# A rebuilt opening: layer 0's wider weights in two transfers, the first half rounded between the two Gelus

## The reference, cut to what matters

```python
x = x + ffn0(conv(x, cond_128, ...))       # x: (128, 32, 512); conv: 9 taps, 4 groups, plus a bias from cond_128
x = x + ffn1(mix(x, cond_128, ...))        # mix: a 32x32 matrix for each sample
# mix: h = gelu(c @ W0 + b0); h = gelu(h @ W1 + b1); att = softmax(h @ W2 + b2)   (8 kernels)
#      agg_w = att * weight (a matrix for each sample);  out = agg_w @ x + att @ bias_k
# ffn: logits = y @ W_router.T; the two best of 8 experts, softmax of the two as weights w
#      h = y @ A.T (8 experts x rank 16);  out = y @ W_base.T + b_base + SCALING * (h * w) @ B
...
```

## Time and profile before

| | |
|---|---|
| median of 3 runs | 398.42 us (396.69 to 398.55) |
| the profiled execution | 398.19 us, span 396.4 us |
| PE busy | 386.1 us (97%), 2789 matmuls |
| DVE, ACT, POOL busy | 280.5 (71%), 207.4 (52%), 226.6 us (57%) |
| share of TensorE on the chain that ended last | 90% |

### The profile page before, as it was taken

The page is one execution under the profiler, slowest core; times in us unless marked ns, Lnnn a source line. Parts: engine busy times, 40 slices in busy tenths (PEclk is TensorE's granted clock), DMA queues, the critical chain, the costliest instruction groups (busy, mean ns, idle before and its releaser), DMA issues.

```text
span 396.4 us, 9115 instructions
## 1 busy us (share of the span) xinstructions
PE 386.1 (97%) x2789; PEld 376.2 (95%) x2789; DVE 280.5 (71%) x983; ACT 207.4 (52%) x529; POOL 226.6 (57%) x199
## 2 busy tenths in 40 slices
PE   7989999999999999999999999999999999999996
PEld 6668999999999999999999999999999999999995
DVE  2787776767667776766777676677767667776764
ACT  3847455555445555544555554455555445555541
POOL 3387765555566565556656555665655566565560
PEclk9999999999999999999999999999999999999999
DMA  7871212222221122222111222212212221121101
GB/s 248 294 157 55 79 49 62 63 73 80 80 80 51 56 66 67 80 80 80 53 54 57 75 80 80 80 53 53 65 67 80 80 80 55 51 70 63 56 27 55
DMA packets 19821, 31.04 MB, mean 78 GB/s; under 512 B 5920, under 2 KB 6208, under 8 KB 19808
## 3 DMA queue, kind: packets, MB, share of 16 engines
q1 hardware_dynamic: 19808, 30.89, 25.2%
HBM read 21.97 MB, written 8.91 MB: 78 GB/s over the span
## 4 chain that ended last, share of the span: by engine, by line
PE 90%; DVE 4%; issue 2%; DMA 1%; ACT 1%; POOL 1%; SPq 0%; DVEq 0%; ACTq 0%; POOLq 0%
PE ps_out L336 33%; PE ps_out L348 22%; PE ps_out L368 11%; PE ps_conv L304 11%; PE ps_mix L384 5%; PE ps_t L316 4%; PE ps_mix L387 2%; DMA pack<-in_pack 1%; PE ps_t L355 1%; DVE yT L632 1%; PE ps_out L355 1%; DVE wb L632 1%; POOL x1b L902 1%; DVE lb_w L648 0%; PE ps_out L395 0%
## 5 line engine op out<-in xcount | busy, mean ns | idle before, releaser
L336 PE MATMUL ps_out<-wa,yT 128*128 128x392 f32 x768 | 152.4, 345 | 1.0 <-ACT yT L483 0.7
L336 PEld LDWEIGHTS ps_out<-wa,yT 128*128 128x128 f32 x768 | 132.2, 188 | 4.4 <-DVE yT L632 1.0
L889 POOL TENSOR_TENSOR x_part<-x,x_part 128x512 fp32r<-128x512 f32 x31 | 40.1, 1293 | 115.2 <-ACT x_part L483 115.2
L348 PE MATMUL ps_out<-wb,yT 128*128 128x256 f32 x768 | 104.4, 285 | 0.2 <-DVE wb L632 0.2
L348 PEld LDWEIGHTS ps_out<-wb,yT 128*128 128x128 f32 x768 | 96.0, 189 | 0.4 <-issue 0.4
L483 ACT ACTIVATE yT<-ps_t 64x256 fp32r<-64x256 f32 x128 | 48.4, 378 | 29.4 <-PE ps_t L316 26.9
L368 PE MATMUL ps_out<-lb_w,hwT 128*128 128x256 f32 x384 | 59.1, 289 | 1.1 <-issue 0.4
L632 DVE TENSOR_TENSOR yT<-ps_t,yT 64x256 fp32r<-64x256 f32 x128 | 53.8, 420 | 3.0
L902 POOL TENSOR_TENSOR x1b<-x,base_bias 128x512 f32<-128x512 f32 x30 | 39.7, 1324 | 26.4 <-DVE res L759 26.4
L520 ACT ACTIVATE wts<-top 128x1 f32<-128x1 f32 x128 | 30.3, 284 | 46.1 <-DVE top L723 46.1
L304 PE MATMUL ps_conv<-x_part,conv_w 128*128 128x256 f32 x384 | 52.1, 285 | 0.0
(11 more groups left out here) (93 smaller groups left out, 478.0 us busy)
## 6 DMA issues: line engine op xcount, KB each, us to landing
x_raw<-in_x_phase SPq DMA_DIRECT2D x32, 260.0 KB, 2.7
x_tok<-in_x_tok SPq DMA_DIRECT2D x32, 256.0 KB, 2.6
out<-res SPq DMA_DIRECT2D x31, 256.0 KB, 2.0
wa_raw<-in_wa SPq DMA_DIRECT2D x2, 784.0 KB, 8.1
wb_raw<-in_wb SPq DMA_DIRECT2D x2, 512.0 KB, 9.2
lb_raw<-in_lb SPq DMA_DIRECT2D x2, 256.0 KB, 6.1
bias<-in_bias SPq DMA_DIRECT2D x2, 256.0 KB, 6.0
scratch<-mix_nat SPq DMA_DIRECT2D x1, 512.0 KB, 2.8
```

The source lines that it names most:

```text
L336: last = mm(out_banks(y, t)[:, 0, 0:AR + DH], yT[y][dp][:, k, :], wa[y][:, wp, k, :], start=(n == 0 and k == 0), stop=(n == len(SPLITS) - ...
L348: last = mm(out_banks(y, t)[:, 1, OUT], yT[y][dp][:, k, :], wb[y][:, wp, k, :], start=(n == 0 and k == 0), stop=False, skip_group_check=True)
L889: g.tensor_tensor(x1_part[LO][:, :], x1[:, :], x1_part[HI][:, :].bitcast(F32), ALU.subtract).then_inc(s["x1l"], 1)
```

## The change: what it does

- **SP:** layer 0's wider weights `wa0` come in two transfers of two k-slices, each with its own semaphore; the other loads stand in another order (the second tile's `x` ahead of the kernels; layer 1's `lb1` and `bias1` and the loads `load_x(2)`, `load_tok(1)` ahead of the mixing matrices). The first tile's four mixing matrices are copied straight from `mix_nat` in SBUF to `mix` (`mix_first`); only the other 31 tiles go through the scratch tensor.
- **ACT:** the high part of `wa0`'s first half is written between the two Gelus, the second half after the softmax's nonlinearity. Exp and Sigmoid become Tanh: softmax by exp(x) = 2/(1 - tanh(x/2)) - 1, and the pair's weights as 1 + tanh, with the factor 2 taken out of the scale (`LORA`). `weigh` has one more instruction, a copy of half the two logits.
- **PE:** `conv(0)` stands before the network on `cond_128`; `mixing_setup` stands inside `first_product(0, 0)`, ahead of its low part; `conv(2)` is done ahead of `first_product(0, 1)`; the column sums come after `second_product(0, 1)`, into other PSUM banks. Step 1 of the steady part is now written out by hand (`stages` begins at 2).
- **DVE and POOL:** the splitting of weights and GpSimd's sums are spread between other work; the semaphores of weights are now one for each array.

```diff
-            for t in range(1, LOOP_FROM):
+            for t in range(2, LOOP_FROM):
...
+                if y == 0:
+                    for ks, landed in ((FIRST_KS, l_wa_first), (LAST_KS, l_wa[0])):
+                        sp.dma_start(wa_raw[0][:, ks, :], d["wa0"][:, ks, :]).then_inc(landed, 16)
...
+            load_x(2)
+            load_tok(1)
+            sp.wait_ge(mix_zero, 1)
             sp.wait_ge(mix_nat_ready, 2)
+            for n in range(SPT):
+                sp.dma_start(mix[n * C:(n + 1) * C, n, :],
+                             mix_nat[n:n + 1, :].rearrange("p (i o) -> p i o", o=C)).then_inc(mix_first, 16)
             sp.dma_start(d["scratch"], mix_nat[:, :]).then_inc(mix_stored, 16)
...
-            keep_busy(10)
+            keep_busy(9)
+            conv(0)
...
-            conv(0)
             kernel_scores()
             turn0(0)
-            keep_busy(4)
+            keep_busy(9)
             turn_probabilities()
             keep_busy(2)
-            mixing_setup()
-            first_product(0, 0)
+            first_product(0, 0, before_low=mixing_setup)
             conv(1)
             second_product(0, 0)
             turn_hw(0, 0)
             turn0(1)
             b_product(0, 0)
-            pe.wait_ge(k_summed, 3)
...
+            conv(2)
+            first_product(0, 1)
+            mix_product(0)
+            second_product(0, 1)
+            column_sums_product()
+            first_product(1, 0, before_low=lambda: turn_hw(0, 1))
...
-                nc.scalar.activation(lb_w[y][:, HI, :], lb_raw[y][:, :], ACT.Copy, scale=SCALING).then_inc(w_hi[y], 1)
+                nc.scalar.activation(lb_w[y][:, HI, :], lb_raw[y][:, :], ACT.Copy, scale=LORA).then_inc(lb_hi[y], 1)
...
                 act.wait_ge(s["top"][y], t + 1)
+                nc.scalar.activation(half_top[y][:, :], top[y][:, 0:2], ACT.Copy, scale=0.5).then_inc(s["half"][y], 1)
+                act.wait_ge(s["half"][y], t + 1)
                 for k in range(2):
-                    nc.scalar.activation(wts[y][:, k:k + 1], top[y][:, 1 - k:2 - k], ACT.Sigmoid, scale=-1.0,
-                                         bias=top[y][:, k:k + 1]).then_inc(s["wts"][y], 1)
+                    nc.scalar.activation(wts[y][:, k:k + 1], top[y][:, 1 - k:2 - k], ACT.Tanh, scale=-0.5,
+                                         bias=half_top[y][:, k:k + 1]).then_inc(s["wts"][y], 1)
...
+            pool.wait_ge(lb_lo[0], 1)
+            pool.wait_ge(l_bias[0], 16)
+            form_xb(0)
+            split_x(2)
```

More of the change, by code:

```diff
@@ L59 @@
 SCALING = 2.0
+LORA = SCALING / 2
+ATT = 2 * N + 2 * E
+FIRST_KS, LAST_KS = slice(0, 2), slice(2, 4)
 HI, LO = 0, 1
@@ L148, in build @@
         top_i = [sb(f"top_i{y}", [P, 8], U32) for y in range(2)]
+        half_top = [sb(f"half_top{y}", [P, 2]) for y in range(2)]
         wts = [sb(f"wts{y}", [P, 2]) for y in range(2)]
@@ L167, in build @@
         conv_w_hi, conv_w_lo = sem("conv_w_hi"), sem("conv_w_lo")
-        w_hi = [sem("w_hi0"), sem("w_hi1")]
-        w_lo = [sem("w_lo0"), sem("w_lo1")]
+        wa_hi, wa_lo, wb_hi, wb_lo, lb_hi, lb_lo = (
+            [sem(f"{n}{y}") for y in range(2)] for n in ("wa_hi", "wa_lo", "wb_hi", "wb_lo", "lb_hi", "lb_lo"))
         zeros_ready, ones_ready = sem("zeros_ready"), sem("ones_ready")
@@ L180, in build @@
         iota_ready = [sem("iota_ready0"), sem("iota_ready1")]
-        for n in ["ar", "top", "wts", "hw", "hwt", "hwh", "hwl", "yh", "yl", "base", "b", "route"]:
+        for n in ["ar", "top", "half", "wts", "hw", "hwt", "hwh", "hwl", "yh", "yl", "base", "b", "route"]:
             s[n] = [sem(f"s_{n}{y}") for y in range(2)]
@@ L278, in step @@
                 load_tok(t + 1)
+            load_x(3)
+            load_tok(2)
             stages(sp, step)
@@ L454, in _ @@
             b_product(0, 0)
-            pe.wait_ge(ones_ready, 1)
-            pe.wait_ge(k_summed, 3)
-            pe.wait_ge(mix_nat_ready, 2)
-            mm(ps_out[1][:, 0, 0:AR + DH], ones[:, :], k_sum[:, 0:AR + DH], start=True, stop=True)
-            mm(ps_out[1][:, 1, OUT], ones[:, :], k_sum[:, AR + DH:AR + D], start=True, stop=True).then_inc(sums_mm, 1)
+            conv(2)
[4 more added lines that the diff above has]
+            first_product(1, 0, before_low=lambda: turn_hw(0, 1))
+            pe.wait_ge(sums_ready, 2)
+            turn0(2)
+            b_product(0, 1)
+            second_product(1, 0)
             stages(pe, step)
@@ L603, in _ @@
             turned0(1, 1)
+            act.wait_ge(mix_first, 16 * SPT)
+            split_mix(0)
             split_x1(0)
-            act.wait_ge(mix_loaded, 16 * SPT)
-            split_mix(0)
-            split_x(2)
+            high_wb(1)
+            weigh(0, 1)
+            save_cross(0)
+            turned1(0)
+            save_sums()
+            pass_bias(0)
+            act.wait_ge(mix_loaded, 16 * SPT)
+            split_mix(1)
+            split_x(3)
+            turned_hw(0, 1)
+            turned0(2, 0)
+            turned0(2, 1)
+            split_x1(1)
+            weigh(1, 0)
+            pass_bias(1)
+            high_lb(1)
             stages(act, step)
@@ L837, in _ @@
             conv_out(1)
-            low_lb(0)
+            low_wa_part(1, FIRST_KS, 1)
             turned_hw(0, 0)
+            turned0(1, 0)
             middle(0)
-            turned0(1, 0)
             turned0(1, 1)
-            low_wa(1)
+            conv_out(2)
+            low_wa_part(1, LAST_KS, 2)
+            choose(0, 1)
+            gate(0, 1)
+            sum_mixed(0)
+            turned1(0)
+            low_wb(1)
+            turned_hw(0, 1)
+            choose(1, 0)
+            middle(1)
+            turned0(2, 0)
+            turned0(2, 1)
+            gate(1, 0)
+            low_lb(1)
             stages(dve, step)
```

190 lines of the change are left out of this document (107 added, 83 removed).

## The result

The changed kernel takes **393.01 us** (median of 4 executions, 392.60 to 393.24), against 398.49 for the kernel before beside it (4 executions, 396.69 to 400.10). The ratio is 0.9876, with a 95% interval of 0.9849 to 0.9903: 1.0 to 1.5% faster.

The account below looks back on a forecast made before the run. TensorE, always behind itself, bounds the kernel, so only an earlier `conv(3)` counts: 398.19 - 3.3 (opening) + 0.2 (halving copy at the end) = 395.1 us; own range 394.0 to 396.4, eight in ten between 393.5 and 397.4.

Parts of the forecast that it names:

- What bounds the kernel: Whole run: TensorE waits only on itself at 11.545 us a tile, so the opening counts only through the start of `conv(3)`.
- The opening: Up to `conv(3)`: it starts at 42.3 instead of 45.57 us, 3.3 us earlier.
- The first product: `first_product(0, 0)` starts at 13.8 us, after ScalarE's four copies of the turned tile.
- `conv(0)`'s new place: Opening, TensorE: `conv(0)` follows nine products of zeros at once, at most 2.62 us, ending at 7.9; no separate price.
- the 2.14 us of mixing setup: Opening, TensorE: setup that stood before the first product now fills time in which VectorE makes the low parts.
- The split of `wa0`: Opening, ScalarE: rounding `wa0` in two halves costs nothing; the second Gelu's loss is saved behind the Tanh.
- The table loads: Opening, ScalarE: two vanishing loads of 1.28 us each cost nothing before, since ScalarE sat idle after each.
- The waits: Opening, TensorE, up to `conv(3)`: remaining waits total 3.0 us, against 5.6 before.
- Column sums: Opening: TensorE newly waits 1.4 us for GpSimd's late `k_sum`, bounds 0 and 2.4.
- The halving copy: Every tile's `weigh`: 0.25 us, covered with 0.5 to spare, costing 0.2 at the end; rival not covered, 402 to 403, 4%.
- The clock: Opening: 1.2 GHz level lasts to 8 us; until 13.5 the start is 1.6 later; rival staying low, 396.5 to 397, 6%.
- VectorE and GpSimd taking turns: Whenever both work in SBUF, the later is blocked; rival that waits move to GpSimd, 396.6 to 397.4, 20%.

## Why the prediction was right, and where its sum was off

The direction and the opening's size held; the time came out 2.1 us below the sum and just outside the range.

- **What bounds the kernel.** Right: the steady tiles show TensorE alone in the chain, and what the opening gave at `conv(3)` reached the end. The failed step is the one that only the start of `conv(3)` counts, with the tile unchanged at 11.545 us. The tile fell to 11.4875, worth 1.60 us, because the change moves SBUF buffers. This is nearly all of the 1.9 us by which the spans differ more than the forecast of 3.1.
- **The opening, 3.3 us forecast, 3.49 measured.** That the two are so close is in part luck: the first product came 0.5 us early, and the 28.78 us from there to `conv(3)`, less the prediction's 25.5 of work, leave 3.3 us of waits against 3.0.
- **The first product, 13.30 and not 13.8.** The prediction followed ScalarE's queue to the four copies of the turned tile. With the higher clock in time for the network's first pair (it ended at 7.91, not 8.6) those copies ended at 12.95, 0.85 early. The path had a step missing: VectorE's rounding of `wa0`'s first half and its links behind the Tanh, which hold TensorE's turn of `att_m` until 12.71, with zeros behind it. And 13.30 is one draw of a time that differs by a microsecond between executions (last section).
- **The parts of the opening.** `conv(0)`'s new place stands in the prediction's layout without a price of its own; in the new queue, by one execution, it is the largest single part, 2.53 us at `conv(3)`. Moving the 2.14 us of mixing setup is worth about 0.4, since the probabilities have to be there first. The split of `wa0`, priced at nothing, gives 0.3 at the first product. These parts overlap with each other and with the next, and do not add up to 3.49. No run undoes SP's new order of loads.
- **The table loads.** That they cost nothing before was read off the idle time and was not tested in the old queue. In the new queue Exp and Sigmoid would cost 1.55 us, nearly all of it through the load ahead of the first weighing.
- **The waits.** Column sums: 1.01 instead of 1.4, with the cause named; moving both sums took it away. Ahead of `mix_product(0)`, 0.4 predicted, the chain shows 0.1 at most (its first matmul takes 0.22 us there, 0.12 in a steady tile); whether `conv(2)` in front, the copies straight from SBUF or GpSimd's new order took away the rest of the 1.36 of before, no run tells. `b_product(1, 0)`: its six matmuls drawn out to 1.37 us, where a steady tile's take 0.86; the wait was put down to the routing of tile 2, and was layer 1's rounding in front of that routing. `b_product(0, 0)`: 0.3 instead of 0.4. What is left of the 3.3, about 1.3 us, lies in no wait that the prediction lists, but in products that each run 0.1 to 0.3 us longer than in a steady tile (`conv(2)` is followed after 1.65 us, where a steady tile's convolution is after 1.45).
- **The halving copy.** Covered in the steady tiles, with 0.39 us to spare in place of 0.5. At the end it costs the 0.2 that was forecast: with equal addresses the stretch behind `conv(31)` is 27.77 us (the changed kernel with the old layout) against 27.58 before, and 27.67 against 27.48 (the kernel before with the new layout). The net 0.09 has 0.1 of the shorter tiles in it.
- **The clock.** The higher level came before the network's first product at 7.53, whose pair takes 0.38 us in place of 0.80; 8 us was assumed, 6 the bound. It came within `conv(0)`, whose matmuls follow each other at 0.21 us up to 6.75 and at 0.12 from 6.93 on.
- **VectorE and GpSimd taking turns.** The rows agree with the prediction's reading: 2.31 against 1.56 for `k_sum`, 2.02 against 1.29 for a sum of 512. The Trainium skill (SBUF — State Buffer, Who interferes with whom) has this as its rule, and these rows are in line with it. So these two engines meet in SBUF too, and not only through semaphores.

## What to carry to other kernels

In a kernel bound by TensorE, a change in the list of SBUF buffers is a change in its own right: measure the steady tile apart from the opening, and compare an edit against a control that keeps the addresses. Price an edit of the opening from the new queue and not from the old one: a load or a convolution that seemed to cost nothing where it stood can be worth 1 to 2.5 us once the work around it has moved. When a wait is to be removed, find the last instruction in its chain that waits for other engines, and move work ahead of that one; one sum moved into idle time ahead of the others only lengthened GpSimd's later waits. An engine that is in time on one path can hold up another: VectorE's rounding in front of the softmax's links set the first product, not ScalarE's copies. The lowest median, 391.82 us with both of GpSimd's sums moved, is 1.3% under the kernel before (0.9 to 1.8%), which the times do not tell from the changed kernel's 1.2%.

## What the runs showed of the hardware beyond that

- The same matmuls in the same order, with no wait in the chain, take 11.48 to 11.55 us a tile depending on where their operands lie in SBUF, and one kernel alternates between the two lengths by tile. No granted clock explains it: the windows grant 1.00 in the steady tiles of both kernels.
- Openings that are alike up to there differ from execution to execution: `conv(0)`, right behind nine products of zeros, took between 1.60 and 2.54 us in the profiled executions with the changed kernel's queue, and the first product started between 12.60 and 13.61. So a single profile tells the start of `conv(3)` only to about half a microsecond; the way from the first product to `conv(3)` repeats better, 28.60 to 28.82 us in five kernels that leave that stretch alone or nearly so (the changed one, `wa0` whole, `x_part` moved, `yT` moved, one sum moved).
